# Two attentions with 8-wide heads: values and row sums in interleaved rows, brought apart by transfers

## The chip, the cores and the metric

The kernel runs on one core of one Trainium2 chip. The metric is the device time of one execution in microseconds (us). The core has a matrix engine (TensorE, in the profile PE for the matmuls and PEld for the weight loads), a vector engine (VectorE, DVE), an activation engine (ScalarE, ACT), a general engine (GpSimd, POOL) and an engine that issues transfers (SyncE, SP). They run their own instruction lists and meet only at semaphores.

## The reference

A block of two layers over x[16, 256, 128]: `x = x + attention(xn) * silu(ffn(xn))`, with xn the layer norm of x, once with a windowed attention and a mixture of experts, once with a full attention and two local-attention layers. The change touches the two attentions. Both have 16 heads of 8 columns:

```python
# layer 0: windows of 64 with the window before, slope bias        # layer 1: all 256 keys, relative bias
qkv = x @ w_in.T ; q, k, v = split(qkv)                            Q, K, V = x@Wq.T+bq, x@Wk.T+bk, x@Wv.T+bv
scores = q k^T / sqrt(8) + slopes * delta   (masked)               scores = Q K^T / sqrt(8) + rel_bias
p = softmax(scores) ; o = p @ v2 ; out = o @ w_out.T               out = (softmax(scores) @ V) @ Wo.T + bo
```

## The kernel before

The core works through stages, each a block of its own: `front` (layer norm, router logits), `window_attention` (layer 0), `experts`, `normalise`, `bias_attention` (layer 1), `inner_layers`. All engines wait for each other between two blocks. `experts` and `inner_layers` are untouched.

Both attentions are pipelines over **units**. A tile is 128 queries; there are 32 tiles, two a batch. A unit is 1,024 score columns of a tile: 8 heads x 128 keys in layer 0 (2 units a tile, 64 in all), 4 heads x 256 keys in layer 1 (4 units a tile, 128 in all). A unit passes these places:

- PE `score` (L601, L899): once for two units, four steps ahead of the rest
- DVE `add_bias` (L701, L1019) adds the table, DVE `row_max` (L705, L1023)
- POOL `shift` (L552, L831) subtracts the maximum, ACT `exp` (L676, L972)
- PE `transposes` (L609, L907): 8 transposes into PSUM banks 4 and 5
- ACT `keep_probT` (L681, L977) copies them to SBUF; only then may the next unit's transposes write the banks
- PE `sums` (L629, L926): probabilities times values, into bank 6, head by head in the four column groups of the array

The order on each engine is fixed: every engine runs the same loop over **steps**, step s doing the transposes and the copy of unit s, and the loops say what else goes where. Odd jobs use bank 7 one after another (`aux_ps`, `aux_free`): transposing x, projecting q and k, projecting v, the output product.

How the softmax is divided by its row sum differs. In layer 0, `sums` has a second kind of product (L633): for each head the probabilities times a tile of ones (`ones`), 128 columns wide, which puts the row sum of every output row beside it in columns 128 to 255 of bank 6. DVE `normalise` (L710, L712) takes the reciprocal from there and multiplies bank 6 with it into `oT`; the next tile's `sums` wait for that (L616). In layer 1, columns of ones stand in `V` beside the values (the tile is 40 wide: 8 values, then zeros or ones), so one product gives values of even heads and sums of their neighbours in one half of bank 6 and the reverse in the other. ACT `keep_sums` (L981) copies both halves to `both`. A job 'd' on PE (L882) multiplies `both` with a permutation (`pick`) that brings each sum to the row of its value, DVE takes the reciprocal (L1030), POOL `scale` (L838) multiplies both halves, 256 columns, and a job 'y' on PE (L887) has two accumulating products, one for each half with its masked output weights (`wO`); DVE adds the bias (L1032). 'd' stands at step 1 and 'y' at step 3 of the tile's following four steps; `scale` goes before `shift` ten units after the tile's first.

In layer 0 the output product of batch i-4 rides on the job 'xy' of batch i (L580), and ACT copies it out (L658). Per batch of four steps the PE order is: step 0 score, v, transposes, sums; step 1 xy, transposes, sums; step 2 score, qk, transposes, sums; step 3 transposes, sums. `between` puts router work of layer 0 into DVE at steps 4, 12, 20, 28 and 36 (L249 to L293).

SP issues no transfer in layer 0's attention. In layer 1's it first issues the inner layers' weights, then five copies of finished rows to DRAM (L810).

Of the kernel before, what the change touches and what calls it, by code (L numbers as in the profile page):

```python
# [9 lines left out]
ALU = mybir.AluOpType  # L10
# [286 lines left out]
def front(nc, t, ps, X, Y, ident, wgu, wd, sel, experts_loaded, skew, attn, route):  # L297
# [4 lines left out]
    with ExitStack() as c:  # L302
# [9 lines left out]
        wnat = sb("wnat", [P, 4, P])  # L312
        desc, lg, st, wT = route["desc"], route["lg"], route["st"], attn["wT"]
        (w_loaded, w_T, ident_loaded, gate_loaded, rel_loaded, rel_ext, rel_out, var_done, seeded, refined, own_rows, other_rows, gate_T, gate_sb, x_T, x_sb,
         logits, shifted, exped) = map(sem, (
            "w_loaded", "w_T", "ident_loaded", "gate_loaded", "rel_loaded", "rel_ext", "rel_out", "var_done", "seeded", "refined", "own_rows", "other_rows", "gate_T",
# [5 lines left out]
        def _(sp):  # L322
# [3 lines left out]
            sp.dma_start(ident[:, :], t["c_ident"]).then_inc(ident_loaded, 16)  # L326
# [22 lines left out]
        def _(pool):  # L349
            pool.wait_ge(rel_loaded, 16)  # L350
# [5 lines left out]
        def _(pe):  # L356
# [16 lines left out]
            pe.wait_ge(ident_loaded, 16)  # L373
            pe.wait_ge(gate_loaded, 32)
# [8 lines left out]
            pe.wait_ge(w_loaded, 32)  # L383
            for j in range(4):
                last = nc.tensor.transpose(ps[:, 4, j * P:(j + 1) * P], wnat[:, j, :], ident[:, :])
# [4 lines left out]
        def _(act):  # L390
# [13 lines left out]
            act.wait_ge(var_done, 1)  # L404
            inverse_deviations(nc, act, rstd[:, :], var[:, :]).then_inc(seeded, 1)
            act.wait_ge(refined, 1)
# [11 lines left out]
        def _(dve):  # L418
# [6 lines left out]
            variances(nc, dve, stats, mean[:, :], var[:, :], tmp[:, :]).then_inc(var_done, 1)  # L425
            dve.wait_ge(seeded, 1)
            refined_deviations(nc, dve, rstd[:, :], var[:, :], mean[:, :], tmp[:, :], shift[:, :]).then_inc(refined, 1)
# [13 lines left out]
def normalise(nc, name, X, Y, stats, loads):  # L441

    with ExitStack() as c:
        mean, var, rstd, shift, tmp = (c.enter_context(nc.sbuf_tensor(f"{name}_{n}", [P, NT], F32)) for n in (
            "mean", "var", "rstd", "shift", "tmp"))
        var_done, seeded, refined = (c.enter_context(nc.semaphore(f"{name}_{n}")) for n in ("var_done", "seeded", "refined"))
# [6 lines left out]
        @block.scalar  # L453
        def _(act):
            start_ln_exp(nc, act)
            act.wait_ge(var_done, 1)
            inverse_deviations(nc, act, rstd[:, :], var[:, :]).then_inc(seeded, 1)
            act.wait_ge(refined, 1)
            for n in range(0, NT, 2):
                nc.scalar.activation(Y[:, n, :], X[:, n, :], ACT.Identity, bias=shift[:, n:n + 1], scale=rstd[:, n:n + 1])  # L460
            act.drain()

        @block.vector
        def _(dve):
            variances(nc, dve, stats, mean[:, :], var[:, :], tmp[:, :]).then_inc(var_done, 1)
            dve.wait_ge(seeded, 1)
            refined_deviations(nc, dve, rstd[:, :], var[:, :], mean[:, :], tmp[:, :], shift[:, :]).then_inc(refined, 1)
# [5 lines left out]
def window_attention(nc, name, t, ps, ident, Y, S, attn, between):  # L473
# [11 lines left out]
    QG = 4  # L485
    XX = HG // 2
    with ExitStack() as c:
# [8 lines left out]
        ones = sb('ones', [P, QG, 40])  # L496
# [3 lines left out]
        rden = sb('rden', [P, P])  # L500
        oT = sb('oT', [P, 4, P])
        bvo = sb('bvo', [P, 2, P])
        zeroed, aux_ps, aux_free, k_sb, masked, scores, biased, max_done, shifted, exped, p_T, pT_sb, pv, o_sb = map(sem, ('zeroed', 'aux_ps', 'aux_free', 'k_sb', 'masked', 'scores', 'biased', 'max_done', 'shifted', 'exped', 'p_T', 'pT_sb', 'pv', 'o_sb'))
        block = c.enter_context(nc.Block())
        NBL = 32
        NZERO = 5 + 2
        AT = {'xy': -7, 'qk': -6, 'v': 0}
        FIRST = AT['xy']
        DELAY = 4
# [21 lines left out]

        @block.gpsimd
        def _(pool):
            nc.gpsimd.memset(xT[:, :, 0:PAD], 0.0).then_inc(zeroed, 1)
            nc.gpsimd.memset(kM[:, :, :, 0:PAD], 0.0).then_inc(zeroed, 1)
            nc.gpsimd.memset(ones[:], 0.0)
            nc.gpsimd.memset(V[:], 0.0).then_inc(zeroed, 1)
            pool.drain()
            for x in range(QG):
                nc.gpsimd.memset(ones[:, x, 0:D], 1.0).then_inc(zeroed, 1)  # L540
# [13 lines left out]
            def add_bias(i):  # L554
                pool.wait_ge(aux_free, job_of('xy', i))
# [1616 lines left out]
```

## Time and profile before

| | us |
|---|---|
| three runs | 1711.24, 1716.27, 1717.79; median 1716.27 |
| span of the profiled execution (first to last instruction) | 1708.8 |
| layer 0 attention, about | 31 to 262 |
| layer 1 attention, about | 569 to 946 |

The profile is of one execution and gives its span; no other time of that execution is listed beside it, so the median of the runs is the nearest figure for what lies around the span (7.5 us). Busy times of instructions include their latency, so neighbours on an engine overlap by some hundredths of a us. Over the span PE is busy 89%, DVE 77%, ACT 71%, POOL 64%. The granted clock of TensorE is 1.00 through the middle of both attentions.

### The profile page before, as it was taken

Reading aid. Unit: us, or ns where it says so; the run is one execution under the profiler, and the core shown is the slowest. Engines: PE = TensorE matmul, PEld = TensorE weight load, DVE = VectorE, ACT = ScalarE, POOL = GpSimd, SP = SyncE. Lnnn points to the kernel's source line nnn. Section 1 sums busy time; section 2 is a strip of 40 time slices with the busy share of each in tenths; the row PEclk is TensorE's granted clock in tenths of the full one; section 3 lists DMA queues with packets and bytes.
Section 4 is the critical chain, followed back from the end, with each engine's and each line's share of the span. In section 5 each row is a group of like instructions: output and inputs, shape, how many; then the busy total and the mean of one; then the engine's idle time right before and its main releaser. Section 6 shows DMA issues by size and latency. Waiting matters only on the chain. (4 is left out here: it accounts for less than half of the span.)

```text
span 1708.8 us, 44008 instructions
## 1 busy us (share of the span) xinstructions
PE 1513.5 (89%) x16988; PEld 1164.6 (68%) x16988; DVE 1319.0 (77%) x2187; ACT 1217.6 (71%) x2065; POOL 1099.4 (64%) x661
## 2 busy tenths in 40 slices
PE   5899996999999499999999578899999999999885
PEld 4677774677776266666666467777777777777774
DVE  5899974555655699999997788887888888888753
ACT  2677774545445488888888378888888888888873
POOL 1777752555555388888887477776676777667614
PEclk8899998999999699999999689999999999999997
DMA  5000000000000500000000001111111110111113
GB/s 174 2 3 3 3 3 15 15 8 7 7 7 1 185 2 2 14 2 14 2 14 11 13 22 31 27 26 27 27 27 27 27 26 22 26 27 27 27 27 105
DMA packets 56837, 44.12 MB, mean 26 GB/s; under 512 B 28152, under 2 KB 47900, under 8 KB 56388
## 3 DMA queue, kind: packets, MB, share of 16 engines
q1 hardware_dynamic: 56644, 41.45, 9.1%
q8 instruction: 133, 2.18, 0.5%
q14 instruction: 60, 0.49, 0.1%
HBM read 17.75 MB, written 4.23 MB: 13 GB/s over the span
## 5 line engine op out<-in xcount | busy, mean ns | idle before, releaser
L831 POOL TENSOR_TENSOR a_prob<-a_prob,a_top 128x1024 f32<-128x1024 f32 x128 | 239.8, 1895 | 48.2 <-DVE a_top L1023 48.2
L1237 POOL TENSOR_TENSOR e_hh<-e_h,e_hh 128x512 fp32r<-128x512 f32 x112 | 144.8, 1293 | 146.6 <-ACT e_hh L1221 145.2
L1506 POOL TENSOR_TENSOR i_qk<-i_qk,i_rt 128x1024 f32<-128x1024 f32 x64 | 152.0, 2375 | 38.1 <-DVE i_rt L1955 33.3
L1516 POOL TENSOR_TENSOR i_qk<-i_qk,i_rn 128x1024 f32<-128x1024 f32 x64 | 122.5, 1915 | 80.5 <-DVE i_rn L1934 80.5
L1019 DVE TENSOR_TENSOR a_prob<-ps,a_table 128x1024 f32<-128x1024 f32 x128 | 149.7, 1211 | 23.4 <-PE ps L899 21.3
L1811 ACT ACTIVATE i_prob<-i_prob,i_top 128x128 f32<-128x128 f32 x512 | 156.4, 391 | 15.7 <-DVE i_top L1943 13.8
L977 ACT ACTIVATE a_probT<-ps 128x1024 f32<-128x1024 f32 x128 | 131.3, 1026 | 44.5 <-PE ps L907 44.5
L1258 DVE TENSOR_TENSOR e_h<-ps,e_sg 128x512 f32<-128x512 f32 x112 | 77.3, 690 | 104.3 <-PE ps L1120 90.4
L907 PEld LDWEIGHTS ps<-ident,a_prob 128*128 128x128 f32 x1024 | 113.2, 141 | 64.2 <-ACT a_probT L977 50.3
L1503 POOL TENSOR_TENSOR i_qk<-i_raw,i_rot 128x1024 f32<-128x1024 f32 x59 | 140.3, 2378 | 24.1 <-issue 24.1
L1208 ACT ACTIVATE e_sg<-ps 128x512 f32<-128x512 f32 x112 | 67.0, 598 | 123.2 <-PE ps L1120 122.4
L1023 DVE TENSOR_REDUCE a_top<-a_prob 128x4 f32<-128x1024 f32 x128 | 149.5, 1209 | 0.0
L907 PE MATMUL ps<-ident,a_prob 128*128 128x128 f32 x1024 | 138.6, 279 | 5.9 <-ACT a_probT L977 1.3
L552 POOL TENSOR_TENSOR a_prob<-a_prob,a_top 128x1024 f32<-128x1024 f32 x64 | 120.2, 1899 | 28.5 <-DVE a_top L705 28.5
L972 ACT ACTIVATE a_prob<-a_prob 128x1024 f32<-128x1024 f32 x128 | 135.4, 1058 | 0.6 <-POOL a_prob L831 0.6
L1776 ACT ACTIVATE i_raw<-ps 128x1024 f32<-128x1024 f32 x64 | 65.6, 1025 | 76.9 <-PE ps L1573 76.7
L1118 PE MATMUL ps<-e_xT,e_wgu_hi 128*128 128x512 f32 x224 | 89.6, 400 | 4.7 <-DVE e_wd_lo L1284 4.7
L1120 PE MATMUL ps<-e_xT,e_wgu_lo 128*128 128x512 f32 x224 | 89.0, 397 | 0.0
L1119 PE MATMUL ps<-e_xT,e_wgu_hi 128*128 128x512 f32 x224 | 88.7, 396 | 0.0
L1652 PE MATMUL ps<-i_wo,i_oT 128*128 128x128 f32 x512 | 71.8, 285 | 18.6 <-ACT i_oT L1822 18.6
L1955 DVE TENSOR_TENSOR i_rt<-ps,i_rot 128x512 f32<-128x512 f32 x128 | 82.0, 682 | 6.0 <-ACT i_raw L1776 6.0
L1652 PEld LDWEIGHTS ps<-i_wo,i_oT 128*128 128x128 f32 x512 | 65.0, 198 | 28.2 <-ACT i_oT L1822 18.7
(305 smaller groups left out, 4369.3 us busy)
## 6 DMA issues: line engine op xcount, KB each, us to landing
i_V<-i_V SPq DMA_DIRECT2D x96, 130.0 KB, 2.3
a_table<-skew_scratch SPq DMA_DIRECT2D x2, 2048.0 KB, 12.4
X<-in_L_attn_x SPq DMA_DIRECT2D x4, 512.0 KB, 6.1
a_table<-in_c_l_table SPq DMA_DIRECT2D x1, 2048.0 KB, 8.3
e_xs<-Y SPq DMA_DIRECT2D x8, 256.0 KB, 2.3
i_ms<-Y SPq DMA_DIRECT2D x16, 128.0 KB, 2.4
i_ms<-Y SPq DMA_DIRECT2D x16, 112.0 KB, 2.4
out_dram<-X SPq DMA_DIRECT2D x7, 256.0 KB, 2.3
```

The source lines that it names most:

```text
L831: nc.gpsimd.tensor_tensor(s, s, top[:, slot].unsqueeze(2).broadcast_to([P, HG, KW]), ALU.subtract).then_inc(shifted, 1)
L907: last = nc.tensor.transpose(ps[:, 4 + b // 4, b % 4 * P:(b % 4 + 1) * P], flat[:, b * P:(b + 1) * P], ident[:, :])
L972: nc.scalar.activation(s, s, ACT.Exp).then_inc(exped, 1)
L977: nc.scalar.activation(probT[:, n % 4].rearrange('p (b n) -> p b n', b=2), ps[:, 4:6, :], ACT.Copy).then_inc(pT_sb, 1)
L1019: nc.vector.tensor_tensor(prob[:, slot].rearrange('p (b x) k -> p b x k', b=2), ps[:, 2 * (n % 2):2 * (n % 2) + 2, :].rearrange('p b (x k) ...
L1023: nc.vector.tensor_reduce(top[:, slot], prob[:, slot], AX.X, ALU.max).then_inc(max_done, 1)
L1237: nc.gpsimd.tensor_tensor(hh[0:n, slot(b, parity), 1, :], h[0:n, slot(b, parity), :], hh[0:n, slot(b, parity), 0, :].bitcast(F32), ALU.sub ...
L1503: nc.gpsimd.tensor_tensor(s, raw[:, T % 2], cosines, ALU.mult).then_inc(cos_done, 1)
L1506: nc.gpsimd.tensor_tensor(s, s, rt[:], ALU.add).then_inc(rotated, 1)
L1516: nc.gpsimd.tensor_tensor(flat, flat, rn[:, T // TPB % 2, T % TPB].unsqueeze(2).broadcast_to([P, 2 * FH, FD]), ALU.mult).then_inc(qk_done, 1)
L1652: last = nc.tensor.matmul(ps[:, 3, 0:P], oT[:, u, :], wo[:, layer(T), u, :], start=(u == 0), stop=(u == 3))
L1811: last = nc.scalar.activation(s, s, ACT.Exp, bias=top[:, T % 2, h:h + 1])
```

## The change

Sums now stand in the rows next to their values in both layers. In `V` each head's 8 values go to every second column, and ones to the columns between them, so the 32 columns that one product loads (they begin at 0, 39, 64 and 103) give values in even rows and sums in odd rows for heads 0 and 2 of a group, and the reverse for heads 1 and 3; the two kinds go to the two halves of bank 6. `ones` and its products, `pick`, the job 'd', `wO` and its masks are gone. ACT `keep_sums` copies both halves to `both` (new in layer 0). Then SP moves the rows with four transfers of 64 partitions x 512 bytes each to `apart`: values to one half, sums to the other, each in its value's row. DVE takes the reciprocal there, POOL multiplies, and one product with the output weights follows, whose rows are put in the new order once before (`wperm`, and copies on POOL at the start of layer 1). Places in the loops: layer 0's reciprocal of tile T at step 2T+6 and its scaling before `shift` of unit 2T+10, the output one batch later (`DELAY` 5); layer 1's reciprocal at step 4T+8, scaling before `shift` of unit 4T+12, 'y' at step 4T+11. Some semaphores are merged (`moments`, `gate_loaded`), which changes no order.

```diff
# front
+            pool.wait_ge(w_loaded, 32)
+            nc.gpsimd.tensor_copy(wperm[:, :].rearrange('p (c d b) -> p c d b', b=2, d=D),
+                                  wnat[:, 3, :].rearrange('p (c b d) -> p c d b', b=2, d=D)).then_inc(w_loaded, 1)
# window_attention
+        def _(sp):
+            for T in range(TILES):
+                sp.wait_ge(both_sb, T + 1)
+                after(sp, apart_sb, 64 * T)
+                after(sp, o_sb, T - 3)
+                for w in range(2):
+                    sp.dma_start(apart[w:P:2, T % 4, 0, :], both[w:P:2, T % 2, w, :]).then_inc(apart_sb, 16)
+                    sp.dma_start(apart[w:P:2, T % 4, 1, :], both[1 - w:P:2, T % 2, w, :]).then_inc(apart_sb, 16)
-            nc.gpsimd.memset(ones[:], 0.0)
-            nc.gpsimd.memset(V[:], 0.0).then_inc(zeroed, 1)
+            nc.gpsimd.memset(V[:], 0.0)
             pool.drain()
-            for x in range(QG):
-                nc.gpsimd.memset(ones[:, x, 0:D], 1.0).then_inc(zeroed, 1)
+            flat = V[:].rearrange('p b v k g (a c) d -> p (b v k g a) (c d)', c=2)
+            for at in (1, 39):
+                nc.gpsimd.memset(flat[:, :, at:at + 2 * D - 1:2], 1.0).then_inc(zeroed, 1)
+            def scale(T):
+                pool.wait_ge(den_sb, T + 1)
+                after(pool, aux_ps, job_of('xy', T // TPB - 2 + DELAY) if T >= 4 else 0)
+                nc.gpsimd.tensor_tensor(oT[:, T % 4, :], apart[:, T % 4, 0, :], apart[:, T % 4, 1, :], ALU.mult).then_inc(o_sb, 1)
-                    after(pe, o_sb, i * TPB + tile)
+                    after(pe, both_sb, i * TPB + tile)
-                                nc.tensor.matmul(ps[32 * g:32 * g + 32, 6, cols], vals[:, 32 * x:32 * x + 32], ...)
-                        for g in range(4):
-                            last = nc.tensor.matmul(ps[32 * g:32 * g + 32, 6, P:2 * P], ones[...], src[:, at:at + P], ...)
+                                out = slice(P * (x % 2) + cols.start, P * (x % 2) + cols.stop)
+                                last = nc.tensor.matmul(ps[32 * g:32 * g + 32, 6, out], vals[:, STARTS[x]:STARTS[x] + 32], src[:, at + cols.start:at + cols.stop], ...)
-                            last = nc.scalar.activation(V[:, par, v, k, :, :, 0:D], ...)
+                            last = nc.scalar.activation(V[:, par, v, k, :, :, 0:2 * D:2], ...)
+            def keep_sums(T):
+                act.wait_ge(pv, (T + 1) * NU)
+                after(act, apart_sb, 64 * (T - 1))
+                nc.scalar.activation(both[:, T % 2].rearrange('p w q -> p (w q)'), ps[:, 6, 0:2 * P], ACT.Copy).then_inc(both_sb, 1)
             for step in range(FIRST, LAST):
+                T, at = divmod(step, NU)
+                if at == 0 and 2 <= T < TILES + 2:
+                    keep_sums(T - 2)
-            def normalise(T):
-                ...
-                nc.vector.reciprocal(rden[:, :], ps[:, 6, P:2 * P])
-                dve.drain()
-                nc.vector.tensor_tensor(oT[:, T % 4, :], ps[:, 6, 0:P], rden[:, :], ALU.mult).then_inc(o_sb, 1)
+            def denominators(T):
+                dve.wait_ge(apart_sb, 64 * (T + 1))
+                nc.vector.reciprocal(apart[:, T % 4, 1, :], apart[:, T % 4, 1, :]).then_inc(den_sb, 1)
# bias_attention: the same transfers on SP, with the copies to DRAM put between them, and
+            pool.wait_ge(w_loaded, NWL)
+            nc.gpsimd.tensor_copy(spread(apart[:, 0, 0, :]), paired(wnat[:, 3, :])).then_inc(zeroed, 1)
+            pool.wait_ge(b_loaded, NBL)
+            nc.gpsimd.tensor_copy(spread(apart[:, 0, 1, :]), paired(bvo[:, 0, :])).then_inc(zeroed, 1)
             nc.gpsimd.memset(V[:], 0.0)
-                    nc.gpsimd.tensor_tensor(oT[:, T % 2], both[:, T % 2], den[:, T % 2].unsqueeze(1).broadcast_to([P, 2, P]), ALU.mult)
+                    nc.gpsimd.tensor_tensor(oT[:, T % 4, :], apart[:, T % 4, 0, :], apart[:, T % 4, 1, :], ALU.mult)
-                scale(n - 10)
+                scale(n - 12)
+            pe.wait_ge(zeroed, 2)
-                elif kind == 'd':
-                    ...
-                    for w in range(2):
-                        last = nc.tensor.matmul(ps[:, 7, 0:P], pick[:, w, :], both[:, T % 2, w, :], start=w == 0, stop=w == 1)
-                    for w in range(2):
-                        last = nc.tensor.matmul(ps[:, 7, 0:P], oT[:, T % 2, w, :], wO[:, w, :], start=w == 0, stop=w == 1)
+                    last = nc.tensor.matmul(ps[:, 7, 0:P], oT[:, T % 4, :], wT[:, 3, :], start=True, stop=True)
```

## Rows read from the trace of the kernel before

**Rows 1.** Windows: length, busy us of PE, PEld, DVE, ACT, POOL; clock; DMA share, GB/s
```profile
180.00:220.00 40.00, 39.71 (x873) 29.50 (x871) 36.45 (x38) 30.90 (x50) 29.24 (x16) 1.00 0.01 3
700.00:800.00 100.00, 93.83 (x1124) 66.89 (x1124) 92.53 (x90) 82.42 (x108) 83.17 (x51) 1.00 0.02 7
```
**Rows 2.** Timeline of ACT in layer 0: start, us, instruction, idle before
```profile
132.55 1.03 ACT L681 ACTIVATE a_probT<-ps 128x1024 f32<-128x1024 f32 x1
...
134.69 0.39 ACT L658 ACTIVATE S<-ps 128x256 f32<-128x256 f32 x1
135.26 1.03 ACT L681 ACTIVATE a_probT<-ps 128x1024 f32<-128x1024 f32 x1 [0.19 <-PE ps L609]
...
139.26 1.03 ACT L681 ACTIVATE a_probT<-ps 128x1024 f32<-128x1024 f32 x1 [0.21 <-PE ps L609]
...
141.47 1.02 ACT L681 ACTIVATE a_probT<-ps 128x1024 f32<-128x1024 f32 x1 [0.24 <-PE ps L609]
...
145.50 1.03 ACT L681 ACTIVATE a_probT<-ps 128x1024 f32<-128x1024 f32 x1
```
**Rows 3.** Timeline of the weight loads in one half of layer 0's sums
```profile
135.16 0.27 PEld L629 LDWEIGHTS ps<-a_probT,a_V 128*32 128x32 f32 x16 [0.17 <-issue]
...
135.35 0.19 PEld L633 LDWEIGHTS ps<-a_probT,a_ones 128*32 128x32 f32 x8
...
136.18 0.23 PEld L601 LDWEIGHTS ps<-a_kM,a_qT 32*64 32x64 f32 x16 [0.20 <-issue]
```
**Rows 4.** Timeline of DVE in layer 0, one pair of units
```profile
137.35 0.29 DVE L712 TENSOR_TENSOR a_oT<-ps,a_rden 128x128 f32<-128x128 f32 x1
137.55 2.35 DVE L701 TENSOR_TENSOR a_prob<-ps,a_table 128x1024 f32<-128x1024 f32 x2
...
139.82 2.33 DVE L705 TENSOR_REDUCE a_top<-a_prob 128x8 f32<-128x1024 f32 x2
```
**Rows 5.** Timeline: two transfers issued by SP one after the other
```profile
560.48 0.43 SPq L142 DMA_DIRECT2D a_wnat<-in_L_attn_Wk  x1
560.95 0.42 SPq L142 DMA_DIRECT2D a_wnat<-in_L_attn_Wv  x1
```
**Rows 6.** DMA issues: count, KB each, median us from issue to landing
```profile
i_V<-i_V SPq DMA_DIRECT2D x96, 130.0 KB, 2.3
```
**Rows 7.** Timeline in layer 1: two copies a batch apart, and the wait before 'y'
```profile
701.07 1.03 ACT L977 ACTIVATE a_probT<-ps 128x1024 f32<-128x1024 f32 x1 [0.23 <-PE ps L907]
...
709.24 1.02 ACT L977 ACTIVATE a_probT<-ps 128x1024 f32<-128x1024 f32 x1 [0.24 <-PE ps L907]
709.25 0.73 POOL L838 TENSOR_TENSOR a_oT<-a_both,a_den 128x256 f32<-128x256 f32 x1
...
710.12 0.68 PE L887 MATMUL ps<-a_wO,a_oT 128*128 128x128 f32 x4 [0.92 <-POOL a_oT L838]
...
712.93 1.03 ACT L977 ACTIVATE a_probT<-ps 128x1024 f32<-128x1024 f32 x1 [1.73 <-PE ps L907]
...
723.15 1.03 ACT L977 ACTIVATE a_probT<-ps 128x1024 f32<-128x1024 f32 x1 [0.23 <-PE ps L907]
```
**Rows 8.** Timeline: ends of both attentions
```profile
259.31 0.96 DVE L710 RECIPROCAL a_rden<-ps 128x128 f32<-128x128 f32 x1 [2.87 <-PE ps L633]
...
261.21 0.38 ACT L658 ACTIVATE S<-ps 128x256 f32<-128x256 f32 x1 [2.57 <-PE ps L580]
...
939.77 0.38 ACT L981 ACTIVATE a_both<-ps 128x256 f32<-128x256 f32 x1 [1.20 <-PE ps L926]
...
944.15 0.29 DVE L1032 TENSOR_TENSOR S<-ps,a_bvo 128x128 f32<-128x128 f32 x1 [2.18 <-PE ps L887]
```
**Rows 9.** Line L819: ones in layer 1's V, 256 elements each
```profile
L819 POOL MEMSET a_V<- x2: 312/349/386, 571.9 to 572.1; 128x256 f32 x2
```
**Rows 10.** Timeline: a DVE instruction with two SBUF inputs beside a POOL instruction
```profile
95.11 1.90 POOL L552 TENSOR_TENSOR a_prob<-a_prob,a_top 128x1024 f32<-128x1024 f32 x1 [1.00 <-DVE a_top L705]
96.07 1.22 DVE L275 TENSOR_TENSOR r_wdense<-r_lg,r_first 128x256 f32<-128x256 f32 x1
```

More of the change, by code:

```diff
@@ L562, in _ @@
                     mask_keys(i)
+                T, r = divmod(n - 10, NU)
+                if r == 0 and T >= 0:
+                    scale(T)
                 shift(n)
-                i, r = divmod(n + 2, U)
+            for T in range((UNITS - 10 + NU - 1) // NU, TILES):
+                scale(T)
         @block.tensor
@@ L807, in _, with keep_rows @@
             ends = (8, 16, 24, 30, TILES)
-            for a, b in zip((0,) + ends, ends):
+            def keep_rows(a, b):
                 sp.wait_ge(aux_free, job_of('y', (b - 1) // TPB, (b - 1) % TPB))
                 sp.dma_start(kept[:, a:b, :], S[:, a:b, :]).then_inc(spilled, 16)
+            for T in range(TILES):
+                sp.wait_ge(both_sb, T + 1)
+                after(sp, apart_sb, 64 * T)
+                after(sp, o_sb, T - 3)
+                for w in range(2):
+                    sp.dma_start(apart[w:P:2, T % 4, 0, :], both[w:P:2, T % 2, w, :]).then_inc(apart_sb, 16)
+                    sp.dma_start(apart[w:P:2, T % 4, 1, :], both[1 - w:P:2, T % 2, w, :]).then_inc(apart_sb, 16)
+                if T - 2 in ends:
+                    keep_rows(([0] + [b for b in ends if b < T - 2])[-1], T - 2)
+            keep_rows(24, 30)
+            keep_rows(30, TILES)
             sp.wait_ge(spilled, 16 * len(ends))
@@ L844, in _ @@
                     mask_keys(i)
-                scale(n - 10)
+                scale(n - 12)
                 shift(n)
-            for n in range(UNITS, UNITS + 10):
-                scale(n - 10)
+            for n in range(UNITS, UNITS + 12):
+                scale(n - 12)
         @block.tensor
@@ L979, in keep_sums @@
                 act.wait_ge(pv, (T + 1) * NU)
[L980 removed]
+                after(act, apart_sb, 64 * (T - 1))
                 nc.scalar.activation(both[:, T % 2].rearrange('p w q -> p (w q)'), ps[:, 6, 0:2 * P], ACT.Copy).then_inc(both_sb, 1)
@@ L1026, in job, with denominators @@
                 dve.wait_ge(aux_ps, n + 1)
-                if kind == 'd':
-                    T = i * TPB + tile
-                    after(dve, o_sb, T - 1)
-                    nc.vector.reciprocal(den[:, T % 2, :], ps[:, 7, 0:P]).then_inc(aux_free, 1)
-                else:
-                    nc.vector.tensor_tensor(S[:, i * TPB + tile, :], ps[:, 7, 0:P], bvo[:, 1, :], ALU.add).then_inc(aux_free, 1)
+                nc.vector.tensor_tensor(S[:, i * TPB + tile, :], ps[:, 7, 0:P], bvo[:, 1, :], ALU.add).then_inc(aux_free, 1)
+            def denominators(T):
+                dve.wait_ge(apart_sb, 64 * (T + 1))
+                nc.vector.reciprocal(apart[:, T % 4, 1, :], apart[:, T % 4, 1, :]).then_inc(den_sb, 1)
             for step in range(FIRST, LAST):
@@ L1035, in _ @@
                     job(a, kind, i, tile)
+                T, at = divmod(step - 8, NU)
+                if at == 0 and 0 <= T < TILES:
+                    denominators(T)
                 n = step + AHEAD
```

136 lines of the change are left out of this document (53 added, 83 removed).

## The prediction

> **What bounds the kernel now.** The windows come first, since the busy shares of the page mix stages. In the middle of layer 0's attention PE is busy 39.7 of 40 us and DVE 36.5; in layer 1's PE 94%, DVE 93%, POOL 83%, ACT 82%, all at granted clock 1.00 [rows 1]. So neither attention has one engine far ahead of the rest: whatever leaves PE can be taken over by DVE or by the chain between two engines. Therefore the timelines come second, read by one marker: the start of ACT's copy `keep_probT`, once per unit.
>
> In layer 0 the markers stand at 132.55, 135.26, 139.26, 141.47 and 145.50: gaps of 2.71, 4.00, 2.21 and 4.03, 12.95 us a batch [rows 2]. The reader is to see that they are unequal. 2.21 is the floor of a hand-over: eight transposes, the copy of 1.03, and the next transposes, which may not write banks 4 and 5 before the copy is over. A gap is longer where the step has jobs on PE beside its sums: xy in the first, score with qk in the second, score with v in the last. A half of the sums takes 1.02 us (135.16 to 136.18), and it is hidden in the 2.21 gap, not in the others [rows 3].
>
> In layer 1 a batch of eight units takes 22.08 (701.07 to 723.15). One gap is 3.69 (709.24 to 712.93), and in it PE waits 0.92 for POOL's `scale`, because POOL had two `shift`s and a key mask to do first [rows 7]. Once a batch 'y' is late, and the score behind it on PE too.
>
> **The change part by part.** *Layer 0, sums.* Each half loses its two groups of ones. The values' loads take 0.19 until the ones' begin, or 0.27 as a group by themselves; an idle of 0.17 stands before them [rows 3]. Without ones a half takes 2 x 0.19 + 0.17 = 0.55 to 2 x 0.27 + 0.17 = 0.71, so it saves 0.31 to 0.47. I take 0.40: the first pair of numbers is of loads that the array swallows beside other matmuls, the second of loads that wait for it. It counts in the two gaps of 4.0: 3.60 and 3.63. The 2.21 gap stays. The 2.71 gap would fall to 2.31 by PE, but ACT has its own list there: copy, exp, x copy, output copy run from 132.55 to 134.69 + 0.39, and the next copy may start at about 2.53 [rows 2]. I take 2.55, and 0.02 for the new `keep_sums`. New batch: 12.01, a gain of 0.94. With 14 batches' worth (16, less the ramps at both ends): 13.2 us.
>
> *Layer 0, ACT.* `keep_sums` is new there, two a batch of 0.38 (its price in layer 1) [rows 8], 0.31 behind the overlap. It stands ahead of exp in the two long gaps, where ACT now waits for PE (q and k copies, v copies). The cover is that wait: the longer gaps lose 0.40 by the sums and 0.31 of ACT's room. If the cover is gone, 0.3 a gap, 9 us in all. The strided write of v changes no count; I take nothing, and at most the same again for four copies a batch.
>
> *Layer 0, DVE.* The multiply of 0.29 goes; the reciprocal stays, now from SBUF. A pair costs 0.96 + 2.27 + 2.33 = 5.56 [rows 4, 8], a batch 11.1 of 12.0: not the bound, but with router work in ten of sixteen batches it will be at times. I take back 1 us for it. Before, the reciprocal waited for the sums of the step just past; now it waits for transfers that were begun a pair of units earlier.
>
> *The transfers.* SP issues one in about 0.47 (560.48 to 560.95) [rows 5], and one of 130 KB between parts of SBUF lands 2.3 after its issue [rows 6]. Four of 32 KB: 3 x 0.47 + 2.3 = 3.7 us; bounds 2.3 and, if each began only when the last had landed, 9.2. In layer 0 they begin about 1.3 after a copy's start and must be in when DVE has done its pair, 6.2 after it by my reckoning: slack about 1.2. In layer 1 seven steps of room are more than enough. SP has nothing else to do but five copies to DRAM, whose waits (rows finished long before) end at once; the inner weights are issued before the first tile is ready.
>
> *Layer 1.* 'd' goes: four records on PE. It sat in gaps where ACT's chain (qk or v copies, exp, copy) is as long as PE's, so I count nothing for it; at most 0.6 twice a batch. The reciprocal moves to the DVE slot right after 'y', where DVE waits for the score anyhow. 'y' halves: 0.68 of busy for four records [rows 7], so about 0.3. And its wait goes: `scale` of tile T now stands before unit 4T+12, POOL does it right after the `shift` that 'y' needs anyway. It costs 128 columns instead of 256: from 0.73 for 256 and 1.90 for 1,024 [rows 7, 10], 1.52 ns a column, 0.54. Its new place is behind the key mask and before a `shift` whose exp starts with nearly no slack; I count 0.5 us there as hidden, since exp ends 0.2 before the transposes it shares ACT with. The long gap falls by 0.92 + 0.3 = 1.2, to 2.5, above the floor of 2.21. New batch: 20.9. DVE needs 92.5% of 22.08 = 20.4 [rows 1]: it fits, just. 14 of 16 batches have the wait: 16.8 us.
>
> *Ends and starts.* Layer 0 now ends in reciprocal to output copy, 259.31 to 261.59, 2.3 us [rows 8]. After: copy 0.38, transfers 3.7, reciprocal 0.96, scaling 0.54, two products about 0.5, copy 0.38, handings-over 0.3: 6.8, so 4.5 more; the last tiles' sums no longer wait for DVE, for which I take 1 back: +3.5. Layer 1: from the end of `keep_sums`, 940.15, to 944.44 is 4.3; after, 3.7 + 0.96 + 0.54 + 0.35 + 0.29 + 0.4 = 6.3: +2.0. Nothing hides either: all engines meet behind them. At layer 0's start two memsets of 512 strided elements, twice the two of 256 for 0.64 in all (0.31 and 0.39 with overlap) [rows 9], stand where small ones stood, ahead of the first key mask: +0.6. At layer 1's start the weights' transposes wait for two small POOL copies, while DVE's preparation of `wO` goes: +0.4, between 0 and 1. The weights' copy in `front` ends long before PE uses it.
>
> **Sum.** -13.2 + 1.0 + 0.6 + 3.5 (layer 0: -8.1), -16.8 + 2.0 + 0.4 (layer 1: -14.4): -22.5. The profiled span 1708.8 becomes 1686.3; with the 7.5 by which the median of the runs is above it, 1693.8, say **1694 us**.
>
> **A rule weighed.** In the trace a DVE multiply with two inputs in SBUF, begun at 96.07 while POOL was at work, ended at 97.29, just after POOL's end at 97.01 [rows 10]. The Trainium skill (SBUF — State Buffer, "Who interferes with whom") says that a DVE instruction with two SBUF inputs contends with a GpSimd instruction that reads SBUF, and one with at most one outside its two-port modes does not. By that rule the row is explained and the new reciprocal, one input, is free; it leaves the sum as it is.
>
> **The rivals.**
>
> *The reciprocal is held by POOL.* It now reads and writes SBUF, which no 128-column reciprocal of the trace does. Were it held like the multiply of rows 10, by 97.01 - 96.07 = 0.94, DVE would need 11.1 + 1.9 = 13.0 us a batch in layer 0 and 20.4 + 1.9 = 22.3 in layer 1: nothing is gained, 0.2 x 15 lost in layer 1, and ends and starts (6.5) stay: 1726, slower. It decides from 0.45 a reciprocal in layer 0 and 0.25 in layer 1. For it: POOL is busy three quarters of the time. Against: the row maxima, one SBUF input, run at 1.2 beside POOL [rows 4].
>
> *The four transfers pass one after another.* Then a tile takes 4 x 2.3 = 9.2 us of the queue against 6.0 us that layer 0 has for it: 32 x 9.2 = 294 us in place of about 207, and layer 1 (10.4 a tile) bears it: about 1790. It decides from 6.0 us a tile. Against: 48 pairs of such transfers are in the 96 with median 2.3 [rows 6]. The Trainium skill (the same page, "Can I just issue two DMAs to hit both halves?") says that two at a time gain little over one, they serialize; for bytes that costs here less than the fixed part, and only if the fixed part serialized too would this rival come.
>
> *Layer 0 gives nothing in its middle*, because ACT with its `keep_sums` or DVE takes the place of PE: -22.5 + 12.2 = -10.3, 1706. For it: ACT's room in the long gaps shrinks.
>
> *Layer 1's wait only moves*, POOL's `scale` behind the mask delaying the shift and exp: -22.5 + 16.8 = -5.7, 1711.
>
> *Both give more*: 0.47 a half, and in layer 1 the room of 'd' too (0.4 a batch): -1.9 - 6 - 3: 1682.
>
> **Numbers.** Forecast 0.53, with its own range 1686 to 1702; layer 0's middle gives nothing 0.13; layer 1's wait moves 0.08; both more 0.14; reciprocal held 0.08; transfers in a row 0.04. The measurement can tell about 0.5%, 8.6 us, so faster is below 1707.7. Faster: 0.53 + 0.14 + most of the 0.13 = 0.76, less a little for a forecast that comes short: 0.74. Same: 0.16, slower 0.10. Range: 1682 to 1710, which leaves out the two slower rivals and a little below.
>
> **What would show it.** In layer 0: copies 3.6, 2.2, 3.6 and 2.5 apart; no L633 products; `keep_sums` with no wait on transfers; DVE not waiting for a transfer in the middle. In layer 1: the 3.69 gap at 2.5 with no wait of PE for POOL, others unchanged. Reciprocals at 0.95, the transfers landed within 4 us of the first issue. Wrong would be: waits of DVE on `apart` in the middle, reciprocals well over 1 us, gaps of 4.0 that stay.

## The result and the profile after

The changed kernel takes 1690.85 us (median of 4 runs, 1687.75 to 1694.09), the kernel before in the same group 1713.84 us: ratio 0.9866, 95% interval 0.9843 to 0.9890. In a later group the same two gave 1683.84 and 1714.1: 0.9825 (0.9809 to 0.9842). The forecast was 1694. Every run lies 1.8 us above its own span (here 1694.09 against 1692.3), so the profiled execution of before took about 1710.6. Of the 7.5 that the forecast put on top of the span, 5.7 is only that this execution was quicker than the median.

In the windows of the kernel after (columns as in [rows 1]):

```profile
180.00:220.00 40.00, 38.40 (x736) 28.61 (x736) 38.61 (x36) 35.41 (x63) 35.59 (x25) 1.00 0.09 25
700.00:800.00 100.00, 92.47 (x1150) 64.97 (x1148) 97.65 (x98) 87.47 (x118) 84.65 (x53) 1.00 0.08 25
```

DVE rose from 36.5 of 40 to 38.6 in layer 0 and from 92.5% to 97.7% in layer 1: it has taken PE's place as the fullest engine. The timeline of ACT's copies in layer 0, against [rows 2]:

```profile
139.51 1.04 ACT L701 ACTIVATE a_probT<-ps 128x1024 f32<-128x1024 f32 x1
140.42 0.41 ACT L691 ACTIVATE a_both<-ps 128x256 f32<-128x256 f32 x1
...
142.95 1.03 ACT L701 ACTIVATE a_probT<-ps 128x1024 f32<-128x1024 f32 x1 [0.22 <-PE ps L627]
...
145.16 1.02 ACT L701 ACTIVATE a_probT<-ps 128x1024 f32<-128x1024 f32 x1 [0.24 <-PE ps L627]
...
148.75 1.03 ACT L701 ACTIVATE a_probT<-ps 128x1024 f32<-128x1024 f32 x1
...
151.15 1.04 ACT L701 ACTIVATE a_probT<-ps 128x1024 f32<-128x1024 f32 x1
```

The gaps are 3.44, 2.21, 3.59 and 2.40, together 11.64 instead of 12.95 (11.63 as the markers of the other batches have it). Layer 1, against [rows 7], has one gap changed, 2.31 for 3.69 (709.24 to 712.93 before, a batch 20.69 for 22.08), and no wait of PE for `scale` before its product of two records; the timelines of PE and of ACT:

```profile
700.67 0.39 PE L912 MATMUL ps<-a_wT,a_oT 128*128 128x128 f32 x2
```
```profile
700.87 1.02 ACT L1002 ACTIVATE a_probT<-ps 128x1024 f32<-128x1024 f32 x1 [0.24 <-PE ps L932]
...
703.18 1.03 ACT L1002 ACTIVATE a_probT<-ps 128x1024 f32<-128x1024 f32 x1 [0.35 <-PE ps L932]
```

The groups by line, for reciprocals and one scaling, and the DMA issues, for the transfers:

```profile
L732 DVE RECIPROCAL a_apart<-a_apart 128x128 f32<-128x128 f32 x32 | 30.3, 946 | 13.8 <-DMA a_apart<-a_both 13.4
L1044 DVE RECIPROCAL a_apart<-a_apart 128x128 f32<-128x128 f32 x32 | 30.2, 943 | 3.4 <-DMA a_apart<-a_both 3.4
...
L868 POOL TENSOR_TENSOR a_oT<-a_apart 128x128 f32<-128x128 f32 x32 | 14.7, 458 | 10.7 <-DVE a_apart L1044 10.7
```
```profile
a_apart<-a_both SPq DMA_DIRECT2D x256, 32.0 KB, 1.8
```

DVE waits for a transfer only once in the middle of layer 0 (0.53 at 227.66); the rest of its 13.8 us of waiting in L732 stands behind 242, at the end.

The stages, as markers cut them: POOL's first memset of layer 0, the starts of the first and last copy of transposed probabilities of each layer, the end of each layer's last output row.

| stage, us | before | after | anchor |
|---|---|---|---|
| front, to layer 0's first memset | 30.8 | 38.5 | 30.1 |
| layer 0, to the first copy | 24.5 | 23.3 | 23.2 |
| layer 0, body (first to last copy) | 198.76 | 184.95 | 184.95 |
| layer 0, end | 7.5 | 11.4 | 11.7 |
| to layer 1's first copy | 330.9 | 332.1 | 332.1 |
| layer 1, body | 345.05 | 324.44 | 324.49 |
| layer 1, end | 6.9 | 9.0 | 9.0 |
| inner layers | 764.3 | 768.7 | 764.2 |
| span | 1708.8 | 1692.3 | 1679.7 |

The changed body of layer 0 repeats within 0.1 us over four profiles (184.9 to 185.0), that of layer 1 within 0.9 over ten (324.1 to 325.0). The front and the inner layers do not: one kernel shows 38.5 and 30.1, 768.7 and 764.2. So the bodies and ends are what the experiments are read by; a single total is blurred by some 12 us that the change does not touch.

The body of layer 0 hides a loss. Two batches took 13.94 and 15.62 instead of 11.6. The timeline of the kernel after at the first:

```profile
78.08 1.89 POOL L559 TENSOR_TENSOR a_kM<-a_kT,a_own 128x1024 f32<-128x1024 f32 x1 [1.79 <-ACT a_kT L678]
78.14 2.12 DVE L272 TENSOR_TENSOR r_first<-r_first,r_second 128x256 f32<-128x256 f32 x1
...
80.33 0.95 DVE L732 RECIPROCAL a_apart<-a_apart 128x128 f32<-128x128 f32 x1
...
81.20 2.29 DVE L724 TENSOR_TENSOR a_prob<-ps,a_table 128x1024 f32<-128x1024 f32 x2
...
83.54 0.24 PEld L619 LDWEIGHTS ps<-a_kM,a_qT 32*64 32x64 f32 x16 [2.46 <-DVE a_prob L724]
```

A router addition of 0.43 took 2.12: it began 0.06 after a POOL instruction of 1.89 and ended 0.3 after it. The bias came late, and PE's weights for the score waited 2.46 for it. The second is L283, 1.75, at 104.07. Before, the same two took 0.43 and 0.42, and POOL was not at work when they began.

The second gap grew more than the first (7.58 and 5.96, where 3.59 is usual), though PE waited as long in both, 2.29. The granted clock explains the difference: behind the second wait it stood at its lower level from 109.5 to 112.9, and the score and v took 1.76 and 2.08 where they otherwise take 1.11 and 1.16. The timeline of PE at the second gap, and at the same place of a usual batch:

```profile
109.12 1.76 PE L619 MATMUL ps<-a_kM,a_qT 32*64 32x512 f32 x16 [2.29 <-DVE a_prob L724]
110.81 2.08 PE L606 MATMUL ps<-a_wT,a_xT 128*128 128x128 f32 x8
```
```profile
134.01 1.11 PE L619 MATMUL ps<-a_kM,a_qT 32*64 32x512 f32 x16
135.05 1.16 PE L606 MATMUL ps<-a_wT,a_xT 128*128 128x128 f32 x8
```

That is 1.6 of the 6.35 us that the two gaps lose together. All five profiles with the long gaps show this stretch, each behind the second wait; none without them does.

### The profile page after: what moved, and what is told of

Its sections match the earlier page's. It is cut to its first block and busy times, and to the rows that moved or that the text cites. A ratio compares the mean times of both kernels' runs of the same rounds, so it can differ in the third digit from the quotient of the medians.

```text
span 1692.3 us, 41853 instructions
## 1 busy us (share of the span) xinstructions
PE 1465.0 (87%) x15772; PEld 1128.3 (67%) x15772; DVE 1303.8 (77%) x2149; ACT 1223.6 (72%) x2097; POOL 1105.0 (65%) x693
## 3 DMA queue, kind: packets, MB, share of 16 engines
q1 hardware_dynamic: 77124, 49.86, 11.1%
## 5 line engine op out<-in xcount | busy, mean ns | idle before, releaser
L932 PE MATMUL ps<-ident,a_prob 128*128 128x128 f32 x1024 | 138.4, 278 | 28.1 <-ACT a_probT L1002 25.9
```

Source lines behind the costliest of these rows:

```text
L932: last = nc.tensor.transpose(ps[:, 4 + b // 4, b % 4 * P:(b % 4 + 1) * P], flat[:, b * P:(b + 1) * P], ident[:, :])
```

## The experiments

The runs with the products kept, the additions, the reductions, the eight transfers and 'y' later are single executions and are read by their bodies.

**The anchor**, the changed kernel once more.

> The changed kernel itself, unaltered, as the anchor of this group. Its profile settles one number only: in the first profile of it layer 0 began at 38.5 us instead of 30.9, with TensorE's granted clock at 0.5 over the whole front. Theory A (chance of the execution): the front is at full clock at least in part again and layer 0 begins near 31 us, span near 1686. Theory B (the added copy of the output weights and its wait keep the clock low): the start stays near 38.5, span near 1692.

Measured: 1683.84 us, span 1679.7, layer 0 from 30.1, first copy at 53.32. Theory A. A group of eight small products of the front, in the timeline of PE, first in the kernel after and then in the anchor:

```profile
25.25 1.71 PE L374 MATMUL ps<-r_gwT,r_xT 128*128 128x8 f32 x8
```
```profile
21.31 0.96 PE L374 MATMUL ps<-r_gwT,r_xT 128*128 128x8 f32 x8
```

The records of the granted clock begin in the first trace only at 44.6 us (the page shows 1.00 ahead of them), so the 0.5 that the expectation names stands in no record there; that the clock was at the lower of its two levels, 1.2 GHz, I infer from these times. The run with additions below bears it out: its records show 0.50 from 20 to 40 us, and the same eight products take 1.71 there too. So the slow front is no property of the changed kernel. What decides it stays open: of the 14 profiles of this case nine have layer 0's first copy at 50.9 to 56.1 and five at 61.7 to 62.6; the five are one of the changed kernel and all four with the router's work late. Whether that last is chance is not shown.

**Each layer alone.** Edits: the function `window_attention` with the front's permuted weights, or `bias_attention`, taken from the changed kernel, the rest from the one before (both with the changed front's merged semaphores).

> Only layer 0's part of the change (its attention and the front; layer 1 as before). My theory, from the stretches of the two traces: layer 0 11.2 us shorter, front 0 to +7.6: span 1698 to 1705, ratio to before 0.993 to 0.998. Layer 0's copies 11.63 a batch outside the two batches with stalls. Rival (the two halves of the change help each other, for instance by the clock): less than 5 us from this one alone.

Measured: 1708.34 us, ratio 0.9959 (0.9943 to 0.9976), span of the profiled execution 1702.2; layer 0's body 184.91, its end 11.8. The median fell by 5.8 us, near the rival's less than 5; the body shows the whole gain.

> Only layer 1's part (layer 0 as before; its front with the new counting of signals but without the permuted copy of the weights). My theory: layer 1's body (first to last copy of the transposed probabilities) 324.5 us instead of 345.0, its end 2 longer, -18.5 us, ratio to before 0.989, layer 0's body 198.8 as before. Rival: layer 1 gains less alone, ratio above 0.993.

Measured: 1698.13 us, ratio 0.9929 (0.9907 to 0.9951); layer 1's body 325.02, layer 0's 198.75. Each layer's body is shortened by its own part alone; the ratio of the second came out weaker than I expected, while its body did not (the runs spread over 9.4 us). The two together give 0.9888 against 0.9825 for the whole change in the anchor's group, and 0.9866 in the first. What is missing probably lies in the stages that vary by themselves; with one profile a kernel that is not shown.

**Layer 0: are the ones it?**

```
+ for g in range(4):   # before the values' products of each half, twice
+     matmul(ps[32g:32g+32, 6, 0:P], ones[...], src[:, at:at+P], start=first, stop=False)
```

(`ones` is here a tile of zeros.)

> The changed kernel with layer 0's second group of products kept: per half two groups of four matmuls by a tile of zeros, 128 columns each, added to the same bank, so the arithmetic adds nothing. Everything else of the change stays. Theory A (the gain in layer 0's middle is PE's, from these products): the gaps of 3.44 and 3.59 go back to about 4.0, and the body from 184.95 to 195 to 199 us. Theory B (the gain is DVE's, from the multiplication that left it, or the earlier release of the bank): the body stays below 190 us.

Measured: body 196.64, span 1696.9. The timeline of ACT there:

```profile
142.00 1.02 ACT L707 ACTIVATE a_probT<-ps 128x1024 f32<-128x1024 f32 x1
...
144.71 1.03 ACT L707 ACTIVATE a_probT<-ps 128x1024 f32<-128x1024 f32 x1 [0.19 <-PE ps L629]
...
148.71 1.02 ACT L707 ACTIVATE a_probT<-ps 128x1024 f32<-128x1024 f32 x1 [0.21 <-PE ps L629]
...
150.91 1.02 ACT L707 ACTIVATE a_probT<-ps 128x1024 f32<-128x1024 f32 x1 [0.23 <-PE ps L629]
...
154.94 1.03 ACT L707 ACTIVATE a_probT<-ps 128x1024 f32<-128x1024 f32 x1
```

Gaps of 2.71, 4.00, 2.20 and 4.03: to 0.01 those of before [rows 2]. Theory A: in the steady batch the whole 1.31 is PE's, from these products; the multiplication that left DVE is worth nothing there, and ACT's new `keep_sums`, which this run has, costs nothing. Neither long gap stands in it: its L272 and L283 took 0.42 and 0.43, since POOL was not at work beside them. With the slower PE the router's work costs nothing.

**Layer 0: the router's work.**

```
- if step >= 4 and step % 8 == 4 and step // 8 < 5:
-     between(dve, 1 + step // 8)
+ if step in (60, 62, 64, 66, 68):
+     between(dve, (step - 58) // 2)
```

> The changed kernel with parts 1 to 5 of DVE's router work moved from steps 4, 12, 20, 28 and 36 of layer 0's attention to steps 60 to 68, where DVE has no biases and maxima left and POOL little. Theory A (in the changed kernel single router operations with two inputs in SBUF are held by POOL, 2.12 and 1.75 us instead of 0.43, and with gaps of PE now only 3.6 the late bias stops PE): the two long gaps (5.96, 7.58) become 3.44 to 3.6, 6.4 us back, at most 1 lost at the end: 5.4 us faster than the anchor. Theory B (the long gaps come from the clock's dip or from something else that stays): 0. Theory C (the router's work now ends last and experts wait for it): slower than the anchor by up to 3 us.

Measured: body 178.60, 6.35 less than the anchor's, both long gaps gone, end 11.9 against 11.7. That is theory A, to 0.1. The median, 1685.68, does not show it, and is 1.8 above the anchor's: in this kernel's profile the first copy stood at 61.97, 8.65 later than in the anchor's. Its four runs lie in two pairs, 1682 and 1689; the gain is one of the body, and no total of this run shows it.

Is it the second input, or just more work for DVE? The late-router kernel with three operations added at five steps:

```
+ if part == 6:  # at steps 4, 12, 20, 28, 36
+     for _ in range(3):
+         nc.vector.tensor_tensor(second[:], rest[:], first[:], ALU.add)        # first kernel
+         nc.vector.tensor_reduce(st[:, :], rest[:], AX.X, ALU.max)             # second kernel
```

> The late-router kernel with three extra DVE additions (r_second<-r_rest,r_first, two inputs in SBUF, 256 elements, 0.43 us each where POOL is quiet) at each of the steps 4, 12, 20, 28 and 36 of layer 0's attention; their result is overwritten later. Theory A (a DVE instruction with two inputs in SBUF is held until POOL's instruction is over): several take 1 to 2.2 us, the body of layer 0 grows from 178.6 by 4 to 10 us, more than in the run with reductions. Theory B (only DVE's own load counts): all take 0.43 and the body grows by 0 to 4 us, as with the reductions.

> The late-router kernel with three extra DVE reductions (r_st<-r_rest, one input in SBUF, 256 elements, 0.42 us each) at the same five steps: the same load of DVE without the second input. Theory A: each takes 0.42 and the body of layer 0 stays within 178.6 to 182. Theory B: the same growth as with the additions.

Measured: body 179.54 with the additions, 178.58 with the reductions. The groups by line, DVE, layer 0, first of the additions and then of the reductions:

```profile
L262 DVE TENSOR_TENSOR r_second<-r_rest,r_first 128x256 f32<-128x256 f32 x15 | 10.3, 688 | 0.7
```
```profile
L262 DVE TENSOR_REDUCE r_st<-r_rest 128x32 f32<-128x256 f32 x15 | 6.2, 416 | 0.7
```

The timelines of POOL and DVE, of the additions:

```profile
145.93 1.90 POOL L569 TENSOR_TENSOR a_prob<-a_prob,a_top 128x1024 f32<-128x1024 f32 x1 [0.26 <-DVE a_top L732]
...
146.90 2.21 DVE L262 TENSOR_TENSOR r_second<-r_rest,r_first 128x256 f32<-128x256 f32 x3
```

and of the reductions:

```profile
145.32 1.90 POOL L569 TENSOR_TENSOR a_prob<-a_prob,a_top 128x1024 f32<-128x1024 f32 x1
...
145.92 1.40 DVE L262 TENSOR_REDUCE r_st<-r_rest 128x32 f32<-128x256 f32 x3
```

The reductions run inside POOL's instruction at 0.42 and cost the body nothing. Of the additions the first in each group took 1.21 to 1.22 and ended 0.3 after POOL's, the other two 0.43. So the addition is held and the reduction is not. The second input is the likeliest reason: the two also differ in the operation and in what they write, but the reciprocals, with one input and a full output, are not held either (0.95). I expected 4 to 10 us from it and it cost 0.9: a hold of 0.8 is mostly absorbed by DVE's room. The 6.35 came with holds of 1.7 and 1.3, on top of a longer router part (about 3 us of DVE where my groups have 1.4), just ahead of a reciprocal and the biases, and with the stretch at the lower clock. How much of it is hold and how much the length of the part no run separates.

One input is no safe conduct. The router's copies to bf16 have one input in SBUF and were held too. The groups by line, DVE, of the kernel after, beside POOL, and of the run with additions, where they come late and POOL is quiet:

```profile
L288 DVE CAST r_rounded<-r_wdense 128x256 bf16<-128x256 f32 x3 | 3.6, 1204 | 0.0
```
```profile
L292 DVE CAST r_rounded<-r_wdense 128x256 bf16<-128x256 f32 x2 | 0.5, 229 | 0.0
```

Each of the first three ended 0.14 to 0.16 after POOL's instruction. No gap of PE grew behind them.

**The transfers' slack.** Four more into a spare buffer, ahead of the real ones, in both layers:

```
+ for w in range(2):
+     sp.dma_start(spare[w:P:2, 0, :], both[w:P:2, T % 2, w, :]).then_inc(apart_sb, 16)
+     sp.dma_start(spare[w:P:2, 1, :], both[1 - w:P:2, T % 2, w, :]).then_inc(apart_sb, 16)
```

> The changed kernel with four more transfers of the same size a tile, into a spare buffer, ahead of the four that count, in both layers: by issues of 0.60 the last lands about 6.0 us after the tile's first issue instead of 3.7. Forecast by slack (in layer 0 the reciprocal starts 6.3 us after the copy's end): layer 0's body 185 to 188 us, its end up to 5 us later since the last tiles' transfers stand in a row, layer 1's body within 1 us of 324.5 and its end 2.4 us later. Rival (the transfers are already near the limit): layer 0's body above 195 us.

Measured: layer 0's body 211.57, layer 1's 324.24; the ends 22.8 and 11.6, so 11.1 and 2.6 longer than the anchor's. My forecast was wrong in layer 0, in its body and its end (at most 5), the rival right. SP and DVE in its timeline:

```profile
142.83 0.47 SPq L543 DMA_DIRECT2D a_spare<-a_both  x1
...
147.30 0.60 SPq L547 DMA_DIRECT2D a_apart<-a_both  x1
149.16 0.47 SPq L543 DMA_DIRECT2D a_spare<-a_both  x1
```
```profile
149.13 0.95 DVE L736 RECIPROCAL a_apart<-a_apart 128x128 f32<-128x128 f32 x1 [1.46 <-DMA a_apart<-a_both]
```

I had reckoned only the delay of one tile (6.0 against a room of 6.3). SP starts the next tile only when the last has landed, so the transfers have a period: 149.16 - 142.83 = 6.33 where nothing else disturbs, and layer 0 leaves half of 11.63, 5.8, a tile. A body of 211.6 is 6.6 a tile. The period alone gives 16 of the 26.6 us (32 times 0.5); the rest is not accounted for in full, but the granted clock now falls four times in the body, each time beside a wait of PE of 2.2 to 4.7. The second rival of the prediction named 6.0 a tile as its threshold. The changed kernel, with 3.64, is free and 6.33 is too much; where between them it breaks was not measured, and 5.8 is what layer 0 leaves. Layer 1's body, with 10.35 a tile, feels nothing.

**Two counters**, on top of the late router: SP no longer waits for the tile before.

```
- after(sp, apart_sb, 64 * T)
+ counters = ((apart_sb, 0), (b_loaded, NBL))   # even tiles, odd tiles
```

> The router work late as in the run before, and also the transfers of even and odd tiles counted by two semaphores, so that SP issues a tile's four without waiting until the tile before has landed. In the late-router kernel the last tiles' reciprocals stood 3.6 us apart and the last transfer was issued at 246.15, some 3 us after its rows were ready. My theory: layer 0 ends 2.5 us earlier than there, its middle stays at 178.6 us, layer 1 0 to 1 us less at its end; 1677 to 1685 in all. Rival (two tiles' transfers at once slow each other): landings above 2.5 us and nothing gained.

Measured: 1679.92 us, ratio 0.9815 (0.9790 to 0.9841), the lowest median of all. Body 178.59; layer 0's end 10.2 instead of 11.9 (250.68 - 240.44), 1.7 less, not 2.5, since SP's eight issues of 0.6 now stand in a row. The rival is refuted: the eight landed 1.7 to 1.8 after their issues. By the stages it is 7.8 us better than the changed kernel (6.36 + 1.4); the medians' 3.9 against the anchor is inside the spread of the front, whose first copy stood at 61.85 in its profile.

**Layer 1: what was the gap of 3.70?** The kernel before with one number changed, POOL's `scale` one unit earlier:

```
- scale(n - 10)
+ scale(n - 9)
```

> The kernel before with one edit in layer 1: POOL does scale of tile T before the shift of unit 4T+9 instead of 4T+10, one shift (1.9 us) earlier; products, transfers, 'd' and everything else as before. Theory A (of the change's 1.38 us a batch in layer 1 most is PE's wait for scale): the gap of 3.70 falls to 2.5 to 2.8 and the body from 345.0 to 328 to 333 us, span 12 to 17 us less. Theory B (the removed 'd', the halved 'y' or the reciprocal's new place give it): the gap stays above 3.4, the body above 341. Rival C: POOL now waits for DVE's reciprocal before the shift, exp is late and the gap at step 4T+8 grows: the body longer than 345.

Measured: 1696.3 us, ratio 0.9898 (0.9867 to 0.9929); body 328.24, theory A. Its timeline of ACT across the gap that was 3.70:

```profile
699.89 1.02 ACT L977 ACTIVATE a_probT<-ps 128x1024 f32<-128x1024 f32 x1 [0.24 <-PE ps L907]
...
702.43 1.03 ACT L977 ACTIVATE a_probT<-ps 128x1024 f32<-128x1024 f32 x1 [0.57 <-PE ps L907]
```

2.54, and no other gap of the batch changed. So 1.16 of the 1.38 a batch, and 16.8 of the 20.6 us of the body, need neither transfers nor a new layout of V; with its shorter end, 6.4 us against 9.0, this kernel's layer 1 stands 1.1 us from the anchor's, hardly more than the 0.9 by which one body varies.

The other way to remove that wait, moving 'y' and not `scale` (one run):

```
- for kind, at in (('d', 1), ('y', 3))
+ for kind, at in (('d', 1), ('y', 4))
```

> The kernel before with one edit: layer 1's 'y' one step later, so that POOL's scale stands before it in good time. Nothing else of the change. Theory A (the change's gain in layer 1 is mostly PE's wait for scale): the 3.70 gap falls to 2.5 to 2.8 and the body from 345.0 to 329 to 332 us. Theory B (it is the removed 'd', the halved 'y' or DVE's load that counts): the body stays above 338 us.

Measured: 1789.92 us, body 419.05. Neither theory foresaw it. Its timeline:

```profile
748.08 2.34 DVE L1019 TENSOR_TENSOR a_prob<-ps,a_table 128x1024 f32<-128x1024 f32 x2
...
750.34 2.33 DVE L1023 TENSOR_REDUCE a_top<-a_prob 128x4 f32<-128x1024 f32 x2
...
750.53 0.71 PE L887 MATMUL ps<-a_wO,a_oT 128*128 128x128 f32 x4
...
752.59 0.28 DVE L1032 TENSOR_TENSOR S<-ps,a_bvo 128x128 f32<-128x128 f32 x1
...
752.92 0.70 PE L871 MATMUL ps<-a_xT,a_wT 128*128 128x256 f32 x2 [1.69 <-DVE S L1032]
...
754.09 0.47 ACT L959 ACTIVATE a_kT<-ps,a_bqk 128x256 f32<-128x256 f32 x1 [3.04 <-PE ps L871]
```

'y' now comes while DVE is in its pair; its addition of 0.28 waits until 752.59, the next job of bank 7 waits for that, ACT for the job, and exp stands behind ACT's copies: two gaps a batch of 6.1 and 6.8. The granted clock, 1.00 from 700 to 900 before, is 0.94 on average here: it falls beside waits of PE like these (one of 2.20 ended at 766.21, and the clock fell at 765.9). The run says nothing on the wait's share; the run before it does.

**A longer warming of PE in the front.**

```
- keep_busy(nc, 4, ps[:, 5, 0:2 * P], ident, X[:, 0:2, :])
+ keep_busy(nc, 8, ps[:, 5, 0:2 * P], ident, X[:, 0:2, :])
```

> The changed kernel with eight instead of four keep_busy products at the head of the front, before PE's first transposes (about 3.8 us more of them). In two of five profiles so far TensorE's granted clock stayed at its low level until 44 us and layer 0's first copy came at 61.7 to 62.0 us instead of 53.3 to 55.7. Theory A (whether the clock rises early depends on what PE did before): the runs of this kernel all rise early, first copy at 53.3 to 57.5, spread of the runs below 4 us. Theory B (the time of rising has nothing to do with it): both kinds again, and 3.8 us are added.

Measured: 1687.14 us, runs within 3.1 us, first copy at 53.74, but no faster than the anchor, whose runs lie as close (3.4): the median is 3.3 above the anchor's, where theory B adds 3.8. One profile with an early clock does not decide between the theories: inconclusive.

## Why the prediction was right, step by step

The mechanisms were the ones named, and the direction and the range held in both groups. That the number came out so near is in part luck. By the medians the change gave -23.0 in the first group and -30.3 in the second, by the spans of the profiled executions -16.5 and -29.1; predicted was -22.5. The bodies and ends of the two layers, which repeat, lost 28.5 us (28.1 in the anchor), where the same terms of the prediction add up to -23.5. So the change is worth about 5 us more than predicted. In the first profile the front (+7.7) and the inner layers (+4.4) hid that, which are as short in the anchor as before the change; the first group's median probably holds a part of it. The anchor's median lies below the forecast's own range (1686 to 1702), inside the stated one, and near the rival "both give more" (1682): the halves of the sums and layer 1's gap did give more, 'd' did not. (The 3 us by which that rival's sum goes on after its two terms are of no row.)

*Layer 0's sums.* Predicted was 12.01 a batch, found 11.63. The term "a half saves 0.40" was too small: the four gaps lost 0.31, 0.56, 0 and 0.44, together 1.31 where I had 0.94. From the start of a half's loads to the next group now take 0.59 against the 1.02 of [rows 3], so it saves 0.43; why the gap with qk gave 0.56 is not shown. The timeline of the loads after:

```profile
145.05 0.49 PEld L648 LDWEIGHTS ps<-a_probT,a_V 128*32 128x32 f32 x32 [0.17 <-issue]
145.64 0.23 PEld L619 LDWEIGHTS ps<-a_kM,a_qT 32*64 32x64 f32 x16
```

The idle behind the half, 0.20 in [rows 3], is down to 0.10 (145.54 to 145.64), where I had kept 0.17; and the gap, with xy, that I held to be ACT's at 2.55 went to 2.40. Over 14 batches that is 5 us more than predicted. In layer 0's body the next term cancelled most of it.

*The router's work*, "I take back 1 us for it", is the term that was too small on the other side. It cost 6.35 (the late-router run), against 1.55 in the kernel before (two gaps of 3.34 and 2.63 where 2.21 is usual), so 4.8 net. The prediction read the row that shows the hold [rows 10] and used it only for the reciprocal, though the row is of a router operation. With DVE at 11.1 of 12.0, a hold of 1.7 had nowhere to go. Beside POOL, two SBUF inputs took 2.12 and 1.21 for 0.43, one input 0.42 (reductions) and 0.94 to 0.95 (reciprocals), but 1.07 to 1.45 for 0.23 in the copies to bf16. The rule of the Trainium skill (SBUF — State Buffer, "Who interferes with whom"), as the prediction tells it, agrees with the additions, the reductions and the reciprocals; whether the copies fall under its exception for two-port modes, no run here tells.

*The reciprocals* were not held: 0.946 and 0.943 on average. That rival is refuted. *The transfers* overlap: they are issued 0.51 to 0.64 apart and land 1.8 after their issue in the median (single ones up to 3.6). A tile's period in the end of layer 0 is 3.64, against the 3.7 of the sum, where two errors cancelled: issues 0.47 apart, landing after 2.3. The Trainium skill (the same page, "Can I just issue two DMAs to hit both halves?") has two concurrent DMAs, one at partition 0 and one at partition 64, at only 6% over one: "they serialize". Of the rate of bytes no run here tells; the whole time of these small transfers does not add up, or four would take 7.2 and not 3.64.

*ACT's `keep_sums`* was covered, as predicted (the run with the products kept has it, and the gaps of before); the strided write of V takes 0.29 for 0.28.

*Layer 0's end*, predicted +3.5, found +3.9 (first profile) and +4.1. The nearly right sum hides a missed step: I took one tile's transfers after the last copy, but the last tiles stood in a row behind SP's own wait, and SP issued the last one's at 251.72, 1.4 after its rows were ready (timeline of the kernel after):

```profile
248.08 0.47 SPq L542 DMA_DIRECT2D a_apart<-a_both  x1
...
251.72 0.47 SPq L542 DMA_DIRECT2D a_apart<-a_both  x1
```
```profile
248.05 0.95 DVE L732 RECIPROCAL a_apart<-a_apart 128x128 f32<-128x128 f32 x1 [4.92 <-DMA a_apart<-a_both]
251.69 0.95 DVE L732 RECIPROCAL a_apart<-a_apart 128x128 f32<-128x128 f32 x1 [2.68 <-DMA a_apart<-a_both]
255.33 0.95 DVE L732 RECIPROCAL a_apart<-a_apart 128x128 f32<-128x128 f32 x1 [2.69 <-DMA a_apart<-a_both]
```

*Layer 0's start*, +0.6: POOL reaches its first key mask 0.7 later (6.36 after its first memset, 5.63 before). The -1.2 of the table is no gain that can be read from it: from memset to first copy the four profiles with layer 0 as before have 21.1 to 24.5, the ten with it changed 23.2 to 25.2.

*Layer 1.* Predicted was 1.2 a batch, found 1.38, a body 20.6 shorter where I had 16.8. Its wait was worth 1.16, not 0.92: the 0.92 in [rows 7] is the idle of the products alone, and 'y' begins with its weight loads, which stood idle 1.13 in the timeline before:

```profile
710.09 0.52 PEld L887 LDWEIGHTS ps<-a_wO,a_oT 128*128 128x128 f32 x4 [1.13 <-issue]
```

Half of 'y' and what came with it gave 0.22, for 0.3. 'd' was worth nothing that can be seen, as predicted: the run with `scale` earlier still has it, and its other gaps are those of the changed kernel. Layer 1's end took +2.1 (+2.0 predicted). Its start (+0.4) cannot be read: with what lies between the layers it is +1.2 in the table, but the stretch is 330.9 to 331.5 in the profiles with layer 1 as before and 331.2 to 332.7 in those with it changed.

*The offset.* 7.5 us was put down to what lies around the span; that is 1.8. The rest is how this one execution differs from the median.

## What to carry to other kernels

Where PE waits for an engine that has something else to do first, try the order of that engine's list before a new layout: here one number gave 17 of layer 1's 20.6 us. The removed work counts only in steps where its engine is last, and what it frees makes the next engine tight; then look for everything on that engine that used to have room, above all DVE instructions with two inputs in SBUF, or copies to bf16, beside a busy POOL. Count a wait of PE as more than its idle time if the clock falls behind it. Compare kernels by the stretches that repeat before you believe a total. A chain of transfers with a wait for the one before has a period as well as a delay; compare the period with the time a tile has.

## What the hardware showed that I had not expected

The front of one and the same kernel ends 8 us earlier or later from one execution to another (layer 0's first copy at 53.32 or 61.73), by the speed of PE's products in it, almost a third of what the whole change is worth. A DVE instruction held by POOL ends a little after POOL's (80.26 against 79.97, and 148.11 against 147.83), and where POOL's next follows at once, that is longer too, 2.08 for 1.90 at 79.94. Of two waits of PE of 2.29 in the same kernel one is followed by a fall of the granted clock and the other is not, and the fall costs 1.6. And transfers of 32 KB between parts of SBUF hardly slow one another: the first of a tile's four lands 1.67 after its issue, the others, issued with one or two under way, 1.80 to 1.84 (medians in layer 0).
